# Graph convolutions: gathers of source rows shared within every supertile, one compare per node block, a ring of two one-hot buffers

## The reference, cut to what matters

```
row = concat(edge_index[0], loop); col = concat(edge_index[1], loop)
deg = segment_sum(ones, col);      dinv = 1 / sqrt(deg)
h   = x @ W1                                # then W2 in the second
out = segment_sum((dinv[row] * dinv[col])[:, None] * h[row], col) + b
```

## Time and profile before

| | |
|---|---|
| median of 3 runs | 4370.68 us (4367.48 to 4373.97) |
| the profiled execution | 4369.29 us |
| its span | 4367.5 us |
| busy PE, DVE, ACT, POOL | 3568.2, 3444.2, 2056.7, 2951.8 us |
| granted TensorE clock, mean | 0.906 |

### The profile page before, as it was taken

How to read it: one execution, slowest core, us unless ns; L and a number is a source line. 1 busy time by engine, 2 the same in 40 slices (tenths; PEclk the granted TensorE clock), 3 DMA queues, 4 the chain that set the end, 5 groups by cost and what they waited for, 6 DMA issues and landing times.

```text
span 4367.5 us, 92806 instructions
## 1 busy us (share of the span) xinstructions
PE 3568.2 (82%) x27877; PEld 3016.5 (69%) x27878; DVE 3444.2 (79%) x6087; ACT 2056.7 (47%) x2171; POOL 2951.8 (68%) x2849
## 2 busy tenths in 40 slices
PE   3997999999999699999999957777766666666665
PEld 3995888888888477777777757777755555555554
DVE  7667999999999688888888878888756777566676
ACT  0106999999999599999999900000000000000000
POOL 1325777777777477777777657766437777477776
PEclk9999999999999799999999977777668888688887
DMA  4002111111111321111111111111011111111111
GB/s 51 26 19 24 24 24 24 24 24 24 24 24 23 23 29 31 30 31 30 31 30 31 23 29 30 28 27 25 13 22 34 33 33 33 23 34 33 33 33 24
DMA packets 260307, 121.63 MB, mean 28 GB/s; under 512 B 165614, under 2 KB 222450, under 8 KB 260278
## 3 DMA queue, kind: packets, MB, share of 16 engines
q1 hardware_dynamic: 172470, 90.58, 8.5%
q0 software_dynamic: 87808, 30.68, 7.0%
HBM read 119.25 MB, written 1.78 MB: 28 GB/s over the span
## 4 chain that ended last, share of the span: by engine, by line
PE 31%; POOL 30%; issue 21%; DVE 11%; DVEq 2%; DMA 1%; ACT 1%; SPq 1%; POOLq 0%; ACTq 0%
POOL gb L384 15%; POOL gb L374 15%; PE ps L581 9%; PE ps L597 9%; PE ps L512 7%; PE ps L587 2%; DVE oht L1139 2%; DVE oh L881 1%; ACT v L490 1%; DVE xt L970 1%; PE ps L528 1%; DMA gb<-table,idx 1%; PE ps L703 1%; DVE gb L1174 1%; DVE v L1153 1%
## 5 line engine op out<-in xcount | busy, mean ns | idle before, releaser
L384 POOL DMA_INDIRECT gb<-table,idx x1568 | 1615.6, 1030 | 554.6 <-issue 418.1
L374 POOL DMA_INDIRECT gb<-table,idx x1176 | 1256.4, 1068 | 592.1 <-issue 354.0
L581 PE MATMUL ps<-big,oh 128*128 128x290 f32 (+1 forms) x7840 | 1263.5, 308 | 1.6 <-DVE big L1010 1.6
L581 PEld LDWEIGHTS ps<-big,oh 128*128 128x128 f32 x7840 | 1068.9, 190 | 124.7 <-DVE big L1010 2.2
L597 PE MATMUL ps<-w,ht 128*128 128x320 f32 x3136 | 1008.3, 444 | 95.5 <-DVE xt L970 93.9
L451 ACT ACTIVATE oh<-iota_f,src_n 128x640 fp32r<-128x640 f32 x1372 | 1024.7, 815 | 0.0
L454 ACT ACTIVATE oh<-oh,ones 128x2560 fp32r<-128x2560 f32 (+1 forms) x392 | 849.4, 2167 | 12.7
L597 PEld LDWEIGHTS ps<-w,ht 128*128 128x128 f32 x3136 | 557.3, 191 | 356.7 <-DVE xt L970 165.4
L970 DVE TENSOR_TENSOR xt<-ps,gb 128x640 f32<-128x640 f32 x784 | 642.5, 820 | 90.7 <-PE ps L597 25.6
L703 PE MATMUL ps<-tabb,oht 128*128 128x240 bf16 x3920 | 527.7, 294 | 110.2 <-DVE mk L1209 98.2
L978 DVE TENSOR_REDUCE msg<-xt 128x80 f32<-128x1280 f32 (+1 forms) x392 | 580.4, 1481 | 0.0
(11 more groups left out here) (212 smaller groups left out, 2576.5 us busy)
## 6 DMA issues: line engine op xcount, KB each, us to landing
gb<-table,idx POOLq DMA_INDIRECT x2744, 2.3
eat<-in_eat SPq DMA_DIRECT2D x196, 192.0 KB, 2.4
eat<-vtab SPq DMA_DIRECT2D x147, 256.0 KB
ea<-in_edge_attr SPq DMA_DIRECT2D x98, 64.0 KB, 1.8
idx<-in_dst SPq DMA_DIRECT2D x196, 4.0 KB, 1.5
idx<-in_src SPq DMA_DIRECT2D x147, 4.0 KB, 1.5
ea<-in_edge_attr SPq DMA_DIRECT2D x1, 784.0 KB, 19.4
table<-tabb SPq DMA_DIRECT2D x2, 300.0 KB, 4.4
```

The costliest lines, as they stand in the source:

```text
L374: nc.gpsimd.indirect_dma_start(out=gb[:, b, t, 0:tabw[p]], out_offset=None, in_=tabs[p], in_offset=bass.IndirectOffsetOnAxis(ap=idx[:, b, ...
L384: nc.gpsimd.indirect_dma_start(out=gb[:, b, t, 0:tabw[p]], out_offset=None, in_=tabs[p], in_offset=bass.IndirectOffsetOnAxis(ap=idx[:, b, ...
L581: mm = nc.tensor.matmul(out, oh5[:, b, t, c * P:(c + 1) * P], big[:, b, t, 0:W], start=False, stop=False, skip_group_check=True)
```

## The change

- The constants `GP` = 3 and `PT` = 5 are new: in **every** supertile tiles 0 to 2 are gathered by POOL and tiles 3 to 7 by PE. So there are 98 steps for each convolution in place of 49.
- `oh_b` holds two whole windows of 8 tiles. DVE makes a window's one-hots in one instruction of 1024 elements, in turn in buffer 0 and 1 (`turn`). PE computes the address of each tile's weights in a register, since `turn` is known at run time only.
- The node numbers of the compare are now f16 (`iota_h`, shifted by `MID` so that they are exact), and `dst_f` is shifted likewise, once, ahead of the first convolution.
- DVE's step makes the windows of supertile s, the source one-hots of s+2 (five of 640 elements) and the selection of s+1 (two of 480, one of 240). PE's step gathers s+1 and then sums the windows of s. One semaphore, `sc_done`, tells POOL and DVE that a supertile is summed.
- SP loads indices and residues for each supertile: `load_tail` brings 640 residues in place of 1024.
- `edge_network`, the stage before (`p` = 2), keeps its work; only its helper lost its arguments.

```diff
+GP = 3
+PT = T - GP
+MID = NP_ // 2
-        oh_b = sb("oh_b", [P, 2, T // 2, P], BF16)
+        oh_b = sb("oh_b", [P, 2, T, P], BF16)
...
+            def load_tail(p, b, s):
+                sp.dma_start(vb[:, b, 0:PT * P], vtab[bass.ds(s, 1), GP * P:SUP].broadcast_to([P, PT * P]))\
+                    .then_inc(vb_in[p][b], 16)
...
+                with sp.Fori(1, PAIRS) as i:
+                    for b in range(2):
+                        sp.wait_ge(g_in[p][b], i * 16 * GP)
+                        load_idx(p, b, i * 2 + b)
+                        sp.wait_ge(oht_done[p], (i * 2 + (b - 1)) * NC)
+                        load_tail(p, b, i * 2 + b)
...
+                with pool.Fori(0, PAIRS) as i:
+                    for b in range(2):
+                        pool.wait_ge(sc_done[p], i * 2 + b + 1)
+                        gather(p, b, i + 1, GP)
...
+                def step(s, b, n, ahead):
+                    lo, hi, off = load_window(pe, s)
                     if ahead:
+                        gather_tiles(s + 1, 1 - b)
+                    pe.wait_ge(g_in[p][b], n * 16 * GP)
+                    pe.wait_ge(mk_done[p], s * 3 + 6)
                     with pe.Fori(lo, hi) as c:
                         at = sums_of(c)
+                        turn = pe.snap((off + c) & 1, min_val=0, max_val=1)
+                        pe.wait_ge(ow_ready[p], off + c + 1)
+                        for t in range(T):
+                            oh = oh_b[:, bass.ds(turn, 1), t, :].rearrange("p o n -> p (o n)")
+                            if t < GP:
+                                mm = nc.tensor.matmul(psf[:, bass.ds(at, 3 * D)], oh, gb[:, b, t, 0:3 * D // 2].bitcast(BF16),
+                                                      start=False, stop=False, skip_group_check=True)
+                            else:
+                                for n_ in range(3):
+                                    mm = nc.tensor.matmul(psf[:, bass.ds(at, AW)], oh, mk[:, b, t - GP, n_ * AW:(n_ + 1) * AW],
                                                           start=False, stop=False, skip_group_check=True)
+                        mm.then_inc(ow_used[p], 1)
+                    idle_matmul().then_inc(sc_done[p], 1)
...
+                def window_onehots(s):
...
+                        dve.wait_ge(ow_used[p], off + c + 1)
...
+                        V.tensor_tensor(oh, bc(one_sup(dst_f, s), P), repeat(iota_h[:, bass.ds(c * P, P)], 1, T),
+                                        ALU.is_equal).then_inc(ow_ready[p], 1)
...
+                def step(s, b, n):
+                    window_onehots(s)
+                    if n is not None:
+                        tile_onehots(s + 2, b, n, False)
+                    if n is not None or b == 0:
+                        select_rows(s + 1, 1 - b)
```

More of the change, by code:

```diff
@@ L367, in _, with gather @@
                 split_low(NSUP - 2 + n, n, n)
[L369 removed]
+            def gather(p, b, seen, n):
                 pool.sem_inc(s_step, 1)
@@ L372, in gather @@
                 pool.sem_inc(s_step, 1)
-                for t in range(T):
+                for t in range(n):
                     nc.gpsimd.indirect_dma_start(
@@ L859, in _ @@
             link(V.tensor_tensor(rv, rv, bc(rnf, 3), ALU.mult))
-            def window_onehots(w, s):
-                lo, hi, off = load_window(dve, s)
-                with dve.Fori(lo, hi) as c:
-                    c = nc.s_assert_within(c, 0, NB - 1, skip_runtime_bounds_check_because="a block index out of the window table")
-                    for h in range(2):
-                        dve.wait_ge(oh_used[w][h], off + c + 1)
-                        d = dst_f[:, bass.ds(s, 1), h * 4:h * 4 + 4].rearrange("p o t -> p (o t)")
-                        cols = repeat(iota_f[:, bass.ds(c * P, P)], 1, T // 2)
-                        V.tensor_tensor(oh_b[:, h, :, :], bc(d, P), cols, ALU.is_equal).then_inc(oh_ready[w][h], 1)
             def one_sup(ap3, s):
@@ L1217, in convolution @@
-                source_onehots(p, 0, 0, 0, 4, range(NC))
-                with dve.Fori(0, QUADS) as i:
-                    for k in range(2):
-                        step(i * 2 + k, i, k, True)
-                step(PAIRS - 1, QUADS, 0, False)
+                dve.sem_inc(mk_done[p], 3)
+                if p == 3:
+                    link(V.tensor_scalar(iota_h[:, :], iota_f[:, :], -float(MID), None, ALU.add))
+                    link(V.tensor_scalar(dst_f[:, :, :], dst_f[:, :, :], -float(MID), None, ALU.add))
@@ new lines, in window_onehots @@
+                def window_onehots(s):
+                    lo, hi, off = load_window(dve, s)
+                    with dve.Fori(lo, hi) as c:
+                        c = nc.s_assert_within(c, 0, NB - 1, skip_runtime_bounds_check_because="a block index out of the window table")
+                        turn = dve.snap((off + c) & 1, min_val=0, max_val=1)
+                        dve.wait_ge(ow_used[p], off + c + 1)
+                        oh = oh_b[:, bass.ds(turn, 1), :, :].rearrange("p o t n -> p (o t) n")
+                        V.tensor_tensor(oh, bc(one_sup(dst_f, s), P), repeat(iota_h[:, bass.ds(c * P, P)], 1, T),
+                                        ALU.is_equal).then_inc(ow_ready[p], 1)
@@ new lines, in tile_onehots @@
+                def tile_onehots(s, b, n, first):
+                    if not first:
+                        dve.wait_ge(mk_done[p], s * 3)
+                    V.tensor_tensor(oh_h[:, b, 0:PT, :], bc(one_sup(src_h, s)[:, GP:T], NH), repeat(iota_f[:, 0:NH], 1, PT),
+                                    ALU.is_equal).then_inc(hh_done[p], 1)
+                    if not first:
+                        dve.wait_ge(gm_done[p], s * 3)
+                    dve.wait_ge(vb_in[p][b], n * 16)
+                    for c in range(NC):
+                        V.tensor_scalar(oht[:, b, c, 0:PT * P], vb[:, b, 0:PT * P], pid_c[:, c:c + 1], None,
+                                        ALU.is_equal).then_inc(oht_done[p], 1)
@@ L1223, in _ @@
+                for b in range(2):
+                    step(NSUP - 2 + b, b, None)
             for p in range(2, 5):
```

176 lines of the change are left out of this document (78 added, 98 removed).

## The result

The changed kernel takes **4460.6 us** (median of 4, 4454.47 to 4466.67), and beside it the kernel before takes 4369.35 (median of 4), as it did ahead of the prediction. The ratio is 1.0207, 95% interval 1.0187 to 1.0227: slower by 91 us, where +50 was forecast. Taken again later it was 4465.99 against 4365.81, 1.0234 (1.0217 to 1.0251).

What follows compares the result with a forecast made beforehand. POOL's gathers bound the convolutions; afterwards a ring over three supertiles would: 503 us, plus 34 second windows, 25 clock, 15 ends, is 577 against 551 to 552; +50 us for both convolutions gives 4420 us, range 4325 to 4505.

Steps and rivals of the forecast that it cites:

- the ring: Convolutions: end of supertile s-2 leads through POOL, SP, residues, DVE and PE to end of s+1; 15.4 us, 503 a convolution.
- second windows and clock: Convolutions: 24 supertiles with a second window add 34 us, PE's lower clock 25 us, on top of the ring.
- the six signs: Convolutions: 577 us stretch, POOL busy 310, DVE awaiting residues 60, compare 1.22, clock above 0.84, PE's window over 0.8.
- the ends: Start and end of each convolution, outside its loop: 15 us.
- the one through the compare: DVE to PE: one-hots, selection and window compare, 4.2 us, then PE's window, 1.7 us, all in the ring.
- clock term: PE's 25 gather matmuls take up to 2.5 us more at low clock; 20% of the time assumed, 25 us a convolution.
- the address arithmetic: PE's window: seven weight addresses computed in registers add 0.77 us; 18 matmuls over 0.8 us even at upper clock.
- DVE's row of work: DVE in the convolutions: one-hots, selections and compares sum to 4.49 us a supertile, 440 us a convolution.
- the rival "faster": Convolutions: the ring is shorter, 14.4 us, 525 a convolution, 4317 us; in the limit DVE decides, 4227; chance 0.27.
- POOL and DVE against each other: POOL's gathers: busier DVE may slow them; each 0.1 us adds 0.3 to the ring, 10 us a convolution.
- The f16 rival: DVE's window compare runs at twice the rate, 0.55 us leaves the ring; no change, 4370 us; chance 0.06.
- PE becomes the bound: Convolutions: at low clock PE costs 7.5 us a supertile; half the time there gives 620 us, 4507 in all; chance 0.15.

Runs made afterwards that it cites:

- the halves: Against the changed kernel, window compare split into two of 4 tiles at constant addresses, one buffer and semaphore each: 5338.04 us beside 5321.76, on another chip.

## Why the prediction was right, and where its sizes were off

The forecast was a ring, slower, 4420 us in 4325 to 4505. It came to 4461 where the kernel before takes the 4369 that it was made for. By its steps, the turn of three supertiles in the mean over the 92 turns of 3235 to 3800 us in the profiled execution:

| part of the ring | forecast, us | measured, us |
|---|---|---|
| marker to the first gather's start | 0.76 | 1.18 |
| to the third gather's start | 2.74 | 2.91 |
| to the residues' issue (landing, SP) | 3.1 | 3.29 |
| residues' issue to DVE's one-hots | 2.9 | 3.33 |
| one-hots to the marker (forecast: one-hots, selection, compare, window) | 5.9 | 7.30 |
| second windows and clock (59 us / 98 x 3) | 1.8 | in the row above |
| turn | 17.2 | 18.01 |

- **The ring stands, with one leg of it another than was said.** Five of the six signs that it named were to be seen. The convolution is 595 us (store at 3219.9 to 3814.6) where 577 was said; POOL is busy 317 us and waits for L729; DVE waits 106 us for residues ("60 or more"); the compare takes 1.216 us; the clock is 0.92 and 0.88, above 0.84. And loading the residues a supertile earlier, one edit in SP's queue, gave 151 us back.
- **The terms that were mis-sized are the hops.** Four parts outside of DVE and PE were each too low, marker to gather by 0.42 us, residues by 0.43, the other two by 0.17 and 0.19: 1.2 us a turn together, or 40 us a convolution (1.21 x 98 / 3). In the kernel before such hops lay hidden behind POOL, and each was read there from one instance. The last row went 0.4 the other way (7.30 for 5.9 + 1.8). 0.8 a turn in sum is 27 us; the ends were smaller than the 15 that I took, and +44 a convolution came out for +26.
- **The leg that was wrong is the one through the compare.** The prediction's ring goes from the selection through the compare to the window. The order is right, but no window waited for the compare, as shown under the halves. Between selection and window stands the row gather of the next supertile, 25 matmuls that are ahead of the window in PE's queue and start behind the first selection. The prediction has that row work as PE's load and in its clock term, and puts it at nothing in the ring. In the 69 turns that end in a supertile with one window the path is 1.55 us to the selection, 1.54 to the row gather's start, 3.05 to the window, 0.74 to the marker: 6.88, where 4.2 + 1.7 = 5.9 was said.
- **The sign that failed is the address arithmetic.** I charged 0.77 us for seven address computations in a window and named "over 0.8 us even at the upper clock" as the sign. From the first of the 18 matmuls' start to the last one's end it is 0.78 us in the median of 118 windows, and 0.58 to the last one's start: in proportion no more than the 1.02 us of 24 matmuls without any. The register instructions run beside the matmuls. A window term that was too dear thus stood against a row gather that was missing, and that the sum came out near is luck.
- **DVE's row of work** was put at 4.49 us a supertile; it is 4.56. But the rival "faster" took 480 us a convolution and 4227 in all for its limit, with 25 us of stalls. With the residues ahead, 0.7 us of short waits a supertile are left, 69 us: 98 x 5.26 = 515 us for the loop, and 4315 is what this edit gives.
- **POOL and DVE against each other** was only suspected, and the changed kernel's trace shows it. Of the 282 gathers in 3235 to 3800 us, the 67 that started with DVE idle took 943 ns in the mean, the 65 that started during a selection 943, the 59 during source one-hots 980, and the 60 during a window compare 1518. A gather that starts during a compare ends 0.82 us behind that compare's end in the median, however long the compare had still to run: it is held until the compare is done. The change made the compare a single instruction of 1.21 us, so it holds longer. Taken over all, a gather takes 1125 ns in place of 943, some 0.5 us for the three of a turn (an estimate). It is the compare and not DVE's busy share: in the first long stage DVE is busy 91% and a gather takes 1060 ns. The Trainium skill's "SBUF — State Buffer", section "SBUF: two separate sides", has DVE and POOL share a port pair that one instruction holds to its end, among others a DVE instruction with two inputs in SBUF against a POOL one that reads SBUF. The compare has two inputs in SBUF, the selection has one in PSUM, and the gather reads its indices from SBUF: the trace agrees.
- **The f16 rival** (0.06) is out by measurement, and so is "PE becomes the bound": PE is busy 402 us of 565.
- **What I did not have at all** is that the sign hangs on the chip. The prediction took every price from one chip; on the other chips the change is worth 183 us (5505 - 5322), for a reason that stays open. Later I expected a ratio of 0.98 to 0.99 there, and it was 0.966.

## What to carry to other kernels

When a change takes work off the engine that sets the time, write down the loops of waits that its slack had been hiding: here SP's queue put an early, independent load behind one that waits for the engine that was relieved, and moving that load one place was worth 151 us, more than the 91 that the change had cost. Count each hop between idle engines by its own latency, from many instances and not from one. List everything that stands in an engine's queue ahead of the step on the path, as the row gather did here. Register work on a matmul's address cost nothing here while it was shorter than the matmuls beside it, and most of its length beyond that.

## What the runs showed of the hardware that I had not expected

- PE's sequencer hides one register instruction of 46 ns behind three matmuls (18 matmuls in 0.575 us, first start to last), while three instructions a tile of 36, 36 and 55 ns make 15 matmuls last 1.61 us in place of 0.70.
- POOL starts its first gather 1.09 us behind the marker (median of the 51 supertiles whose earlier gathers had all ended), and further ones with 0.30 us of gap.
- A gather that starts during a DVE compare of 128 x 1024 ends 0.82 us behind the compare's end, and takes 1518 ns in the mean in place of 943.
- A broadcast of 160 KB of residues takes 2.7 us from issue to its last packet in the median, and the 256 KB of before take 2.9: hardly more. The 3.59 of the earlier trace rows goes up to the user's start, in one instance.
- Three of four chips take 26% longer for one and the same kernel (5505 and 4366 us), with transfers as long and with gaps between PE's matmuls that chip 0 does not have; and a change can be 2.1% slower on one and 3.4% faster on the others.
